# Four mixed layers on one core: DRAM buffers with the images innermost, an opening for one image, and a joined stage that begins with its key loads side by side

## What is computed

```python
x = x + L0(gn(x))      # below
x = x + L1(gn(x))      # spectral: rfft2, two complex products in 4 groups, irfft2
x = x + L2(gn(x))      # gate per channel from block means
x = x + L3(gn(x))      # spectral, as L1

# L0: tokens (4, 4096, 512), 8 heads of 64, chunks of CS = 16 tokens
xn = layernorm(tokens) * ln_w + ln_b
XQ, XK, XV = rope(xn @ q_w.T), rope(xn @ k_w.T), xn @ v_w.T
eta = token_idx * sigmoid(xn @ lr_w + lr_b) / 64
def step(W, b, xq, xk, xv, et):               # one chunk, 256 in a row
    Z = xk @ W + b
    grad = ln_l2_backward(Z, xv - xk)
    b_bar = b - tril(et) @ grad
    Zbar = xq @ W - et * tril(xq @ xk.T) @ grad + b_bar
    W -= (last_eta * xk).T @ grad;  b -= sum(last_eta * grad)
    return xq + layernorm(Zbar)
y = (layernorm(outputs of all chunks) * post_w + post_b) @ o_w.T
```

## Time and profile before

| | us |
|---|---|
| median of 3 runs (lowest, highest) | 6241.13 (6234.36, 6241.5) |
| profiled execution | 6242.9 |
| its span | 6241.0 |
| TensorE busy | 5393.6 (86%) |
| VectorE busy | 3919.7 (63%) |
| ScalarE busy | 2368.3 (38%) |
| GpSimd busy | 2385.5 (38%) |
| mean granted clock of TensorE | 0.938 |

### The profile page before, as it was taken

One profiled execution on the slowest core, in us unless ns is written; L12 is line 12 of the kernel. 1 busy time (PEld: TensorE's weight loads), 2 busy tenths in 40 slices (PEclk: granted clock), 3 DMA queues, 4 the chain that ended last, 5 costly groups with the idle time before them and its releaser, 6 DMA issues. The chain is left out here.

```text
span 6241.0 us, 144090 instructions
## 1 busy us (share of the span) xinstructions
PE 5393.6 (86%) x42556; PEld 3821.0 (61%) x42556; DVE 3919.7 (63%) x14026; ACT 2368.3 (38%) x6675; POOL 2385.5 (38%) x3910
## 2 busy tenths in 40 slices
PE   1799999999588888888888888888799999599999
PEld 0344444444267777777777777777666666377777
DVE  5566666666377777777767777777566666544444
ACT  0111111111055555555555555555333333233333
POOL 0244444444255455555545554454122222122222
PEclk9899999999779899989999998999899999799999
DMA  6233333333344444444444444444212221222221
GB/s 246 72 128 120 127 120 127 120 128 120 127 106 119 125 119 123 118 122 118 119 119 121 120 120 120 118 122 126 98 77 87 87 87 45 78 88 87 87 87 70
DMA packets 823279, 693.73 MB, mean 111 GB/s; under 512 B 357224, under 2 KB 758000, under 8 KB 811664
## 3 DMA queue, kind: packets, MB, share of 16 engines
q1 hardware_dynamic: 732304, 542.54, 29.1%
q10 hardware_dynamic: 90240, 142.75, 6.1%
HBM read 402.96 MB, written 282.20 MB: 110 GB/s over the span
## 5 line engine op out<-in xcount | busy, mean ns | idle before, releaser
L1390 PE MATMUL proj_ps<-proj_w_sb,proj_h 128*128 128x512 f32 x3072 | 1345.6, 596 | 0.0
L1390 PEld LDWEIGHTS proj_ps<-proj_w_sb,proj_h 128*128 128x128 f32 x3072 | 577.2, 190 | 743.4 <-issue 716.6
L2195 PE MATMUL scan_ps_y<-scan_o_t,proj_wo_sb 128*128 128x128 f32 x4096 | 648.2, 307 | 2.1 <-ACT scan_o_t L1827 2.1
L1312 DVE SCALAR_TENSOR_TENSOR proj_lin<-proj_ps,proj_rstd,proj_wbias_sb 128x512 f32<-128x512 f32 x384 | 284.5, 748 | 545.8 <-PE proj_ps L1390 544.8
L2195 PEld LDWEIGHTS scan_ps_y<-scan_o_t,proj_wo_sb 128*128 128x128 f32 x4096 | 565.1, 214 | 50.8 <-issue 8.6
L1737 POOL TENSOR_TENSOR scan_b_step<-scan_core,scan_rate_last 128x128 f32<-128x128 f32 x512 | 318.6, 622 | 650.5 <-DVE scan_core L1984 650.5
L1963 DVE TENSOR_TENSOR scan_zg<-scan_ps_z,scan_gain 128x128 f32<-128x128 f32 x512 | 146.1, 285 | 563.1 <-ACT scan_square L1798 518.0
L1798 ACT ACTIVATE scan_square<-scan_ps_z 128x64 f32<-128x64 f32 x1024 | 218.6, 220 | 651.0 <-PE scan_ps_z L2113 645.4
L1791 ACT COPY scan_state_w<-scan_ps_w 128x512 f32<-128x512 f32 x480 | 281.3, 586 | 476.1 <-PE scan_ps_w L2125 455.5
L2125 PE MATMUL scan_ps_w<-scan_step,scan_record 64*128 64x128 f32 x4088 | 386.5, 312 | 12.4 <-DVE scan_step L1989 11.9
L1266 POOL TENSOR_TENSOR proj_gk<-proj_rec,proj_gain_sb 128x256 f32<-128x256 f32 x256 | 181.5, 729 | 554.5 <-DVE proj_rec L1333 554.5
(11 more groups left out here) (290 smaller groups left out, 12327.7 us busy)
## 6 DMA issues: line engine op xcount, KB each, us to landing
scan_record<-records SPq DMA_DIRECT2D x1032, 98.0 KB
records<-proj_rec ACTq DMA_DIRECT2D x128, 784.0 KB, 3.6
scan_k_in<-records SPq DMA_DIRECT2D x266, 128.0 KB
spectra<-fourier_spec SPq DMA_DIRECT2D x16, 2112.0 KB, 6.4
fourier_spec<-spectra SPq DMA_DIRECT2D x16, 2112.0 KB, 8.2
stats_x<-x SPq DMA_DIRECT2D x16, 2048.0 KB, 7.7
proj_h<-x SPq DMA_DIRECT2D x32, 1024.0 KB, 7.1
queries<-proj_q ACTq DMA_DIRECT2D x128, 256.0 KB, 3.7
```

The source lines that it names most:

```text
L1312: v.scalar_tensor_tensor(lin[q][:, n], ps[q][n][:], rstd[k][:, j:j + 1], T.wbias[:, n], ALU.mult, ALU.add).then_inc(lin_sb.sem, 1)
L1390: last = pe.matmul(ps[j % 2][n][:], h[k][:, ct, j * P:(j + 1) * P], T.w[:, n, ct], start=ct == 0, stop=ct == CT - 1)
L2195: pe.matmul(ps_y[:, n], T.wo[:, ct, n * P:(n + 1) * P], o_t[:, ct], start=ct == 0, stop=False)
```

## The change

DRAM buffers: images become the innermost dimension but one, so a step's records of all four images are one transfer (128 rows of 3136 bytes), a group's gradients one (512 bytes a row), and queries, x and y are moved for a whole block of 128 tokens, four images at once. Gradients back are two transfers a tile with rows of 256 bytes, where it was one with 512; records are stored by two transfers a sub-step with rows of 784 bytes, where it was one with 1568. The single blocks of the opening become one, `opening`, with the statistics of image 0 alone; those of image b + 1 are made in the projection stage while image b is projected (`channels`, `image_moments`, `image_variance`, `image_factors`, `next_image`), whose loop body is now a whole image. The pads are written at that stage's start. In the joined stage the constants are loaded by ScalarE, the first keys of the four images go to four places of a query buffer, and VectorE's zeroing stands ahead of the wait for the constants.

```diff
-def prepare_projections(nc, T, d):
...
+def opening(nc, T, d, x_in, group_mean, gn_first):
...
+                sp.dma_start(T.w[:, n], d["wT"][n]).then_inc(w_in[n], 16)
+            for k in range(CT):
+                sp.dma_start(xb[k][:], x_view[k]).then_inc(x_in_sb[k], 16)
+            sp.dma_start(T.wo[:], d["wT"][3]).then_inc(wo_in, 16)
...
+        def _(act):
+            for dst, src in ((vecs, d["vecs"]), (T.lrw[:, :, 0:NH], d["lr_wT"]), (lr_b, d["lr_b_row"].partition_broadcast(P)),
+                             (group_mean, d["group_mean"]), (T.gain, d["ttt_rows"][0].partition_broadcast(P)),
+                             (T.shift, d["ttt_rows"][1].partition_broadcast(P)), (T.ident, d["dft"][8]), (T.pick, d["pick"])):
+                act.dma_start(dst[:], src).then_inc(small_in, 16)
...
+            statistics(0)
+            statistics(1)
...
+            projection(0)
+            statistics(2)
+            statistics(3)
...
+            projection(1)
...
+            projection(2)
...
+                    body(b * groups + g, b * (groups // 2) + g // 2, g % 2, b, g, last and g == groups - 1)
+
+            with eng.Fori(0, images - 1) as b:
+                image(b, False)
...
+        def following(b, g):
+
+            return not isinstance(b, int) and g < CT
...
-                sp.dma_start(h[k][:], x_view[bass.ds(b, 1), :, :, bass.ds(g * 512, 512)].rearrange("o c k n -> (o c) k n")).then_inc(x_loaded[k].sem, 16)
-                sp.dma_start(table[k][:], rope[bass.ds(g * 512, 512), :].rearrange("(j p) e -> p j e", p=P)).then_inc(x_loaded[k].sem, 16)
+                sp.dma_start(h[k][:], x_view[b, :, :, g * 512:g * 512 + 512]).then_inc(x_loaded[k].sem, 16)
+                sp.dma_start(table[k][:], rope[g * 512:g * 512 + 512, :].rearrange("(j p) e -> p j e", p=P)).then_inc(x_loaded[k].sem, 16)
+                if following(b, g):
+                    sp.wait_ge(xs_read.sem, xs_read.at(b, g))
+                    sp.dma_start(xs[:], x_view[b + 1, :, g]).then_inc(xs_loaded.sem, 16)
...
-                    act.dma_start(rec[bass.ds(b, 1), :, bass.ds(g * 512 + j * P, P)].rearrange("o a t n e -> (o t) a (n e)"),
-                                  rec_sb[:, j].rearrange("p (a n) e -> p a (n e)", n=2)).then_inc(rec_out[j].sem, 16)
+                    for n in range(2):
+                        act.dma_start(rec[:, bass.ds(g * 512 + j * P, P), n, bass.ds(b, 1)].rearrange("a t o e -> (o t) a e"),
+                                      rec_sb[:, j].rearrange("p (a n) e -> p a n e", n=2)[:, :, n]).then_inc(rec_out[j].sem, 16)
...
             normalise(0, 0, 0)
+
+            act.wait_ge(init.sem, init.at(0, 1))
+            for a in range(NH // 2):
+                for n in range(2):
+                    act.dma_start(rec[a, TOK + n * P:TOK + (n + 1) * P].rearrange("t n b e -> t (n b e)"), zero[:]).then_inc(pad_out.sem, 16)
             rows_out(0)
...
-            for b in range(B):
-                for n in range(2):
-                    act.dma_start(rec[b, :, TOK + n * P:TOK + (n + 1) * P].rearrange("a t n e -> t a (n e)"), zero[:]).then_inc(pad_out.sem, 16)
...
+            def channels(b, n, j):
+
+                dve.wait_ge(xs_loaded.sem, xs_loaded.at(b * CT + n, 16))
+                dve.wait_ge(chan_sb.sem, chan_sb.at(b, 0))
+                for m in (2 * j, 2 * j + 1):
+                    last = v.bn_stats(stats6[:, n, 6 * m:6 * m + 6], xs[:, 512 * m:512 * m + 512])
+                if j == SUB - 1:
+                    last.then_inc(xs_read.sem, 1)
...
-            def load_record(g, ring, s):
-                for b in range(PB):
-                    sp.dma_start(record[g][ring][:, b, :], rec[PB * g + b, :, bass.ds(s * CS, CS)].rearrange("a t n e -> a (t n) e")
-                                 ).then_inc(rec_in[g][ring].sem, 16)
-
-            def load_keys(b, sc):
+            def load_record(ring, s):
+                sp.dma_start(record[ring][:].rearrange("p b e -> p (b e)"), rec[:, bass.ds(s * CS, CS)].rearrange("a t n b e -> a (t n) (b e)")
+                             ).then_inc(rec_in[ring].sem, 16)
+
+            def load_keys(dst, landed, b, sc):
...
-                    sp.dma_start(k_in[:].rearrange("p (a n) e -> p a n e", n=2)[:, :, n],
-                                 rec[b, :, bass.ds(sc * P, P), n, n * HD:(n + 1) * HD].rearrange("a t e -> t a e")
...
+                    sp.dma_start(dst.rearrange("p (a n) e -> p a n e", n=2)[:, :, n],
+                                 rec[:, bass.ds(sc * P, P), n, b, n * HD:(n + 1) * HD].rearrange("a t e -> t a e")
+                                 ).then_inc(landed.sem, 16)
...
+            for b in range(B):
+                load_keys(q_sb[0][:, b], first_keys[b], b, 0)
             for s in range(2):
-                for g in range(GR):
-                    load_record(g, s, s)
-            for b in range(B):
-                if b:
-                    sp.wait_ge(turn_k.sem, turn_k.at(b, 0))
-                load_keys(b, 0)
-            sp.wait_ge(turn_k.sem, turn_k.at(B, 0))
-            load_keys(0, 1)
-            load_query(0, 0, 0)
+                load_record(s, s)
+            load_keys(k_in[:], k_loaded, 0, 1)
...
                 if scan:
                     if c == 0:
                         for g in range(GR):
                             sp.wait_ge(b_sum_sb[g].sem, b_sum_sb[g].at(s, 0))
-                            for b in range(PB):
-                                sp.dma_start(s_snap[bass.ds(((v * 2 + at.p) * B + PB * g + b) * P, P), :],
-                                             b_sum[g][0][:, b, :]).then_inc(snap_gone[g].sem, 16)
+                            sp.dma_start(s_snap[bass.ds(v * 2 + p, 1), g].rearrange("o p b e -> (o p) (b e)"),
+                                         b_sum[g][0][:].rearrange("p b e -> p (b e)")).then_inc(snap_gone[g].sem, 16)
+
                     for g in range(GR):
-
                         sp.wait_ge(state_ps[g].sem, state_ps[g].at(s, -1))
-                        load_record(g, (c + 2) % RING, s + 2)
-                if at.odd:
-                    tile = at.tile(LEAVE)
...
-                        sp.dma_start(x_sb[b % 2][:], x_view[b, :, :, bass.ds(sc * P, P)]).then_inc(x_loaded[b % 2].sem, 16)
+                    load_record((c + 2) % RING, s + 2)
+                if c == 1 and (scan or p == 0) and (not isinstance(v, int) or v * 2 + p):
+
+                    sp.dma_start(x_sb[1 - p][:], x_view[:, :, bass.ds((v * 2 + p - 1) * P, P)]).then_inc(x_loaded[1 - p].sem, 16)
                 if scan:
...
                         sp.wait_ge(stored_sb[g].sem, stored_sb[g].at(s, 1))
-                        for b in range(PB):
-                            sp.dma_start(grad[PB * g + b, :, bass.ds(s * CS, CS)].rearrange("a t n e -> a (t n) e"),
-                                         stored[g][c % 2][:, b, :]).then_inc(grad_gone[g][c % 2].sem, 16)
+                        sp.dma_start(grad[:, bass.ds(s * CS, CS), :, PB * g:PB * g + PB].rearrange("a t n b e -> a (t n) b e"),
+                                     stored[g][c % 2][:]).then_inc(grad_gone[g][c % 2].sem, 16)
+                if c == 7 and (not isinstance(v, int) or v):
+
+                    sp.wait_ge(y_done.sem, y_done.at(v * 8 + p * 4 - 4, 0))
+                    sp.dma_start(o_view[:, :, bass.ds((v * 2 + p - 2) * P, P)], y_sb[p][:]).then_inc(y_gone[p].sem, 16)
...
-                        sp.dma_start(grad_sb[q][:].rearrange("p (a n) e -> p a (n e)", n=2),
-                                     grad[b, :, bass.ds(sc * P, P)].rearrange("a t n e -> t a (n e)")).then_inc(grad_in[q].sem, 16)
                         for n in range(2):
...
+                            sp.dma_start(grad_sb[q][:].rearrange("p (a n) e -> p a n e", n=2)[:, :, n],
+                                         grad[:, bass.ds(sc * P, P), n, b].rearrange("a t e -> t a e")).then_inc(grad_in[q].sem, 16)
+                        for n in range(2):
...
+                    if c == 3:
+
+                        if isinstance(v, int) and not p:
+                            sp.wait_ge(turn_k.sem, turn_k.at(B, 0))
+                        if not isinstance(v, int):
+                            sp.wait_ge(qb_sb.sem, qb_sb.at(v * 8 + p * 4 - 4, 0))
+                        sp.dma_start(q_sb[p][:].rearrange("p b h e -> p b (h e)"), q_in[:, bass.ds((v * 2 + p) * P, P)].rearrange("b n c -> n b c")
+                                     ).then_inc(q_loaded[p].sem, 16)
+
+                    b, n = (c // 2 + 1) % B, p + 1 + (c // 2 + 1) // B
+                    sp.wait_ge(turn_k.sem, turn_k.at(v * 8 + at.slot + 1 + B, 0))
+                    load_keys(k_in[:], k_loaded, b, v * 2 + n)
...
             v = nc.vector
+            steps.then(dve, v.memset(eps[:], HD * 1e-6))
+            for q in range(2):
+                for b in range(B):
+                    steps.then(dve, v.memset(k_t[q][b][:], 0.0))
+            for q in range(2):
```

(40 more changed lines are left out.)

480 lines of the change are left out of this document (256 added, 224 removed).

## The result

The changed kernel takes 6021.62 us, the median of 4 runs (6017.79 to 6036.71), against 6241.32 before: a ratio of 0.9655 (95% interval 0.9637 to 0.9673). It is 220 us faster; 451 were forecast, and the time lies 12 us above the top of my range (6010). The profiled execution took 6036.7 us with a span of 6034.6, so 206.4 less span than before.

What follows compares the result with a forecast made beforehand. The prediction took the joined stage to be bound by SyncE's issuing, with TensorE close behind. Opening -133, seam -31, joined stage -291 and drain +3 took 6242.9 to 5791, median 5790 us; range 5670 to 6010.

Steps and rivals of the forecast that it cites:

- the sum for the joined stage: Joined stage: SyncE's DMAs per block go from 100 to 53, blocks from 82.0 to 72.9 us, -291 us.
- The four engines: Rival, joined stage: records and stores use four of sixteen DMA engines, which become the bound; 78 us a block, 5954; chance 0.19.
- the late queries: Joined stage: TensorE's longest wait, 195 us in 88 waits for the queries' load, would go.
- the loop's edge: Joined stage, once in two blocks: a 2 us wait and a slot of 22.90 instead of 17.17 us.
- the 22.90 us slot: Joined stage: a slot behind a loop-edge wait, mean clock 0.78, no late queries; cited against the clock staying up.
- the clock stays up: Rival, joined stage: the edge loses its lower-clock stretch; 69.2 us a block, -410, total 5672; chance 0.11.
- Opening: Before the first projection product: 12 of 16 x loads go, first product at 82 instead of 215, -133 us.
- a late small load: Opening: with the pads of zeros, the reason given for the upper bound of 100 on the first product.
- Projection stage: Added statistics, stores and x loads all lie under the matmuls: 0; other end +58 if the cover fails.
- Seam and drain: Between projection and joined stage: pads leave, keys and constants wait less, -31 us; drain after the joined stage, +3.
- Bursts: Rival, joined stage: 1 MB loads landing in 22 us starve the recurrence; 102 us a block, 6722; chance 0.03.

Runs made afterwards that it cites:

- e1: Changed kernel with each step's record load cut in four by pair of heads (outer dimension 32, was 4): 5714.0 us, 69.2 us a block.
- e10: Changed kernel with each step's record load cut in two by heads (outer dimension 2, rows of 3136 bytes): 6919.2 us, 106.4 us a block.
- e9: Changed kernel with each step's record load cut in two by images (outer dimension 4, rows of 1568 bytes): 5903.9 us, 75.0 us a block.
- e4: Changed kernel, SyncE starting after ScalarE's small loads landed, and x for the statistics asked for behind the next h: 5977.6 us.
- e2: Changed kernel with each step's record load cut in four by image (outer dimension 4, rows of 784 bytes): 5929.7 us, 75.9 us a block.
- e3: Kernel before the change with its record loads cut by pair of heads instead of by image (outer dimension 32): 6356.2 us, 85.3 us a block.

## Why the prediction was wrong

**The step that failed is the sum for the joined stage: fewer DMAs "at 0.74 and 0.93 us for records and stores and 0.47 for the others", so "34 us of a block, instead of all of it", and from that 72.9 us a block.** It charges nothing for the time in which the four engines that carry records and stores hold the queue up; the prediction had that term, at 69 to 82 us of transfers, and set it aside. SyncE's DMA rows took 63.8 us of a block and not 34. Their shortest rows sum to 24.3, and 39.5 are hold-up, where it was 11.6 before. The reading that led there, "So the joined stage is bound by SyncE's issuing", was right in the main for the kernel before (72 us of 83.4 were SyncE's own), but the next bound lay within a few us of it: with half of the DMAs gone the rest became longer until the queue was full again, key and snapshot loads among them. e1 shows it by removing the cause: 24 DMAs more, 25 us of SyncE's time less, and 10 us a block gained. e10 shows it from the other side: at e9's number and price of DMAs, 35 us more of hold-up.

**The four engines** were among the rivals, with the right mechanism and nearly the right numbers (69 to 82 us of transfers in a block, a block of 78; measured 79.2). I gave that 0.19. The argument against it was that before the change they "carry as many bytes and more". That was no argument: the kernel before ran at 81.8 us a block, so it showed only that they can do it in 81.8. And SyncE's never waiting, which I took as proof for the issuing, is what a held-up queue looks like too. The share of the records was put too low: their 1024 packets of 3136 bytes took 179 us of engine time a block, 45 on each of four engines, where the prediction has 35 to 38. That the rival's 78 came so near the 79.2 is in part luck, with a range of 69 to 82 behind it. The rival's total, 5954, missed the profiled 6037 by the opening (20 more than forecast), the projection stage (30) and the recurrence (46), with 5 taken back by the seam and 11 by the drain.

**Queries.** That the late queries would go was right, but not what stands behind: the snapshots' load took their place, 15.1 us of waits before, 89.7 now.

**The clock.** TensorE spends 14.9 us of a block at the lower level before, 15.5 after, 1.4 in e1, 50.4 in e10. In these four kernels the lower level goes with the waits for DMAs: 210 us of such waits of TensorE in the stage before, 107 after, none in e1, 579 in e10; before and after it stayed the same although the waits halved, and this is not explained. I had charged about 4 us a block to the loop's edge. In e1 the edge's waits are still there (31.7 us in 14), and the clock hardly falls: the 22.90 us slot of the earlier trace rows was not the edge's doing alone. So the rival "the clock stays up" (69.2 us a block) is what one gets once the four engines are out of the way.

**Opening.** -133 was forecast, -113 came. I had the x loads pace it, with the small loads beside them. In fact the small loads share the engines with 12 MB, and the last of them landed at 36; VectorE waits for all of them before its first statistics. The bounds named "a late small load" with an end of 100, which was short by 2. e4 gives 84.2, against my 82.

**Projection stage.** 0 was forecast, 30.5 came: "h is asked for a whole step before the products that need it" was wrong. SyncE asks for it at 154.93, ScalarE is done with it at 171.1, and the next step's row sums wait 2.25 us for that:

```profile
153.68 0.35 SPq L1212 DMA_DIRECT2D proj_xs<-x  x1
154.93 0.38 SPq L1208 DMA_DIRECT2D proj_h<-x  x1
155.74 0.81 SPq L1209 DMA_DIRECT2D proj_rope<-rope  x1
```

```profile
171.15 1.07 PE L1453 MATMUL proj_ps_rows<-proj_h,proj_lrw_sb 128*32 128x512 f32 x8 [2.25 <-ACT proj_h L1226]
```

It happens three times an image, 21.1 us in 9 waits; 18 us more at the lower clock than before (23.5 against 5.5), at half speed, account for the other 9. The 0.605 us statistics on VectorE cost nothing, as forecast: e4 keeps them and loses nothing.

**Seam and drain** were right in kind: -35.6 for -31 (SyncE's first load of the joined stage to the first recurrence matmul is 28.0 us, not 33), and -7.7 for +3. **Bursts**: a load of x of 1 MB landed in 12.7 us (forecast 22, threshold 17), and in 6.7 in e1, so its length too was the four engines' doing.

**Open.** Why the changed kernel, with the fewest DMAs, is slower than e9 and e2 on the same four engines (79.2 against 75.0 and 75.9). The rows are longest there (3136 bytes), and hold-up of small DMAs is largest: 1.76 us for a snapshot load, 1.07 in e9, 0.69 in e2. The hold-up does fall step by step with the rows, 39.5, 27.9 and 19.6 us a block; the block does not, because the price of more DMAs rises against it: the shortest rows sum to 24.3, 29.4 and 37.7, and both together are 63.8, 57.3 and 57.3. Why longer rows hold the queue up more is not shown. A queue that holds a number of rows rather than of bytes would fit; no run tests it.

## What to carry to other kernels

An issuing queue that never waits may be short of its own time or held up by the engines behind it: compare the duration of one and the same small DMA at its shortest and at its median. Where they agree (0.37 and 0.38 us for a key load before), the queue's own time counts and fewer DMAs can help, but only as far as the next bound; where the median is far above (0.98 after), the queue is held up, and the transfers that hold it have to be changed. Look at the outer dimension of each large transfer in DRAM before merging transfers: 2 and 4 tied it to as many engines here, 32 did not. But each more DMA costs about 0.6 us of the queue: with the records off the four engines, 77 DMAs a block gave 69.2 us and 125 gave 80.3.

When loads are moved to another queue or another place, ask what lands ahead of what: two edits of order, which removed no byte, were worth 44 us.

## What the runs showed that I had not expected

The number of engines follows the outer dimension down to 2, and two such transfers don't share out over four engines: 0.13 of the DMA share and 52 GB/s in e10. One transfer on few engines holds up small ones for other engines through the common issuing queue: a key load occupied SyncE for 0.37 us at best, 0.98 at the median of the changed kernel and 6.5 at worst. And a DMA's price for SyncE follows its shape: one record load took 0.32 us at the shortest with an outer dimension of 32, and 0.50 to 0.55 with 2 or 4, whether its rows had 784 or 3136 bytes; e3 and e10 have 64 rows a load both, so it isn't their number.
